# Shared-expert rows as stored high and low parts, a reordered opening and a split last product, in an adaLN block with a top-2 mixture of experts

## The chip, the cores and the metric

The kernel runs on one core of one Trainium2 chip. The metric is the device time of one execution in microseconds (us). A core has five engines that run their own instruction streams and wait for each other by semaphores: TensorE (PE, matrix products; its weight loads are shown as PEld), VectorE (DVE), ScalarE (ACT), GpSimd (POOL), and SyncE (SP), which here only issues DMA transfers. PE's results land in eight PSUM banks of 128 x 512 fp32; everything else that an engine reads is in SBUF.

## The reference, cut to what matters

Everything is fp32 and is computed with nearly fp32 accuracy.

```
x: 2048 x 512;  mod = silu(c) @ wmod -> sa, ca, ga, sb, cb, gb (512 each)
h  = layernorm(x) * (1 + ca) + sa
x  = x + ga * (tanh(h @ B.T) @ C.T + D * h)                 # 256 states
h  = layernorm(x) * (1 + cb) + sb
scores = sigmoid(h @ gate_w.T); pick 2 of 8 experts by scores + bias
w      = the two scores, normalised to sum 1
routed = sum of w_k * W2_k(silu(h @ W1_k) * (h @ W3_k))      # hidden width 352
shared = sw2(silu(h @ sw1.T) * (h @ sw3.T))                  # hidden width 704
out = x + gb * (routed + shared)
```

The shared expert of width 704 is computed as two experts of width 352, A and B, so that A, B and the eight routed experts all have the same shapes.

## The kernel before, in words

A tile is 128 rows (tokens); there are NT = 16 tiles, in NP = 8 pairs. Each fp32 product is made of three products of rounded operands: with a = ah + al and b = bh + bl (`high` is a Copy that rounds to fp32r, `low` is the subtraction of what is left), it is ah*bh + ah*bl + al*bh. So whatever goes into a product needs its high and its low part in SBUF.

The work has three stages.

*Stage A* (function `body`, iterations `it` = 0 to 10). A software pipeline over the pairs: in iteration `it`, pair `it` is normalised, pair `it-1` is transposed (`turn_t`) and its states are computed (`states`), pair `it-2` gets the output of the attention-like part (`attention`), is normalised again and its rows are written to DRAM (`hs`), pair `it-3` is transposed (L1037), split into high and low parts (`xah`, `xal`; `high_a` on ACT, `lows_a` on DVE) and goes through expert A, and pair `it-4` is routed: its rows are fetched back from `hs` and scattered to the DRAM tensor `xs`, where each expert has its own region (`scatter`, four indirect DMAs of POOL). Iteration 3 is the first with an expert in it; what comes before it (L1088 to L1111) is called the opening here.

*Steps* (function `step`, section letters B, S, C). Every step takes one tile through one expert of width 352: `up`, 24 products of 352 columns into banks 2 and 3; `down` of the step before, 9 products of 512 columns; and `turn_g`, three transposes of the hidden values. ACT computes the silu (L873) and the high part of the turned hidden values (L881), DVE their product with the other half (`gbuf`, L1653) and the low part (L1668). In the order of PE the `down` of a step is thus one step late, which gives ACT and DVE the time of an `up`.
- B: four steps, tiles 0 to 3 through shared expert B, while the routing table is finished (`table_rows`, `table_rest` on DVE, semaphores `s_row` and `s_tab`) and the first routed expert's weights come in.
- S: 36 steps (for these inputs) over the routed rows in `xs`; the results are written to the DRAM tensor `ys`.
- C: twelve steps, tiles 4 to 15 through shared expert B. Each one ends with the output: POOL gathers the tile's two rows per token from `ys` (`gather`), DVE combines them with the shared result and x (`finish`, four operations), SP stores. Tiles 0 to 3 are combined beside them in `rowb` (`gather_first`, `finish_first`). I number the C steps k = 0 to 11.

In all 52 steps the tile's rows come by a DMA from DRAM (`hs` in B and C, `xs` in S) into `xin`; PE transposes them (`turn`, four transposes, L929), ACT takes the high part (L722), DVE the low part (L1387).

The weights: POOL fetches each expert's 4.3 MB twice (once to be kept as `raw`, once rounded, `whi`) and computes the low part (L536), into one of two slots.

SP's queue is one list in program order: a DMA that waits holds up all behind it. At the end of stage A this list is: tiles 0 and 1 for B, the rows of pairs 6 and 7 for the scatter (`rows_of_pair`), tiles 2 and 3 for B, and then the rows of the first routed tiles, which wait for all scatters (L450 to L457).

## Time and profile before

| | us |
|---|---|
| median of three runs | 567.3 (567.28 to 568.34) |
| the profiled execution, its own time | 568.31 |
| its span, first to last instruction | 566.6 |
| PE busy in the span | 545.8 |
| DVE, POOL, ACT busy | 301.5, 263.2, 181.1 |

The granted clock of PE was 0.994 of full speed over the span. Stage A ends and B begins at about 205 us of the span, S begins at about 233, C at about 477, and the last store is issued at 564.2. A busy time is the sum of the instructions' own times with overlaps taken once; PE works on several instructions at a time, so what one costs is read from the distance between starts, and not from its length.

### The profile page before, as it was taken

To read this page: it belongs to the slowest core of one execution; us is meant where nothing else is said; L and a number is where in the kernel's file an instruction comes from. 1 tells how busy PE (TensorE), PEld (TensorE's weight loads), DVE (VectorE), ACT (ScalarE), POOL (GpSimd) and SP (SyncE) were. 2 spreads that over 40 slices of the span, in tenths; PEclk is the share of its full clock that TensorE was granted. 3 is DMA by queue.
4 is the path that set the end of the run, shared out by engine and by line. 5 is a ranking of instruction groups with operands and counts; after the bars stand their busy time and mean duration, and the time that the engine had idled before them with its cause. 6 is when DMAs were issued, how large, how long until landed. Compare 5 with 4: busy or idle time off the path is not lost.

```text
span 566.6 us, 11166 instructions
## 1 busy us (share of the span) xinstructions
PE 545.8 (96%) x3184; PEld 490.3 (87%) x3185; DVE 301.5 (53%) x631; ACT 181.1 (32%) x347; POOL 263.2 (46%) x221
## 2 busy tenths in 40 slices
PE   8997799999999999999999999999999999999995
PEld 3666688988999999899999999999999999889994
DVE  3788776696677667632222222222222222479886
ACT  1444346345443442133222322232222322222210
POOL 2599886677667456443053430053535100245531
PEclk9998999999999999999999999999999999999998
DMA  8999245331332597566255754267676222367744
GB/s 306 395 330 333 75 153 219 131 111 74 111 122 103 175 331 292 185 225 223 95 185 203 278 183 178 90 215 267 214 259 206 91 74 74 112 208 221 225 157 137
DMA packets 41113, 107.19 MB, mean 189 GB/s; under 512 B 4224, under 2 KB 4224, under 8 KB 41088
## 3 DMA queue, kind: packets, MB, share of 16 engines
q1 hardware_dynamic: 28288, 54.44, 27.3%
q0 software_dynamic: 12800, 52.43, 26.8%
q8 instruction: 14, 0.23, 0.2%
q14 instruction: 11, 0.09, 0.1%
HBM read 76.19 MB, written 30.67 MB: 189 GB/s over the span
## 4 chain that ended last, share of the span: by engine, by line
PE 82%; POOL 6%; DVE 5%; issue 3%; DMA 2%; ACT 1%; SPq 0%; DVEq 0%; POOLq 0%
PE bank L946 15%; PE bank L947 14%; PE bank L948 14%; PE bank L962 8%; PE bank L960 8%; PE bank L961 8%; PE bank L929 5%; PE bank L967 4%; PE bank L898 2%; PE bank L900 2%; PE bank L899 2%; DMA x_all<-wmod 2%; POOL x_all L552 1%; POOL tmpa L544 1%; POOL tmpa L549 1%
## 5 line engine op out<-in xcount | busy, mean ns | idle before, releaser
L946 PE MATMUL bank<-whi,thi 128*128 (+1 forms) x416 | 139.0, 334 | 0.0
L947 PE MATMUL bank<-wlo,thi 128*128 (+1 forms) x416 | 134.6, 324 | 0.0
L948 PE MATMUL bank<-whi,tlo 128*128 (+1 forms) x416 | 134.3, 323 | 0.0
L536 POOL TENSOR_TENSOR wlo<-raw,whi 128x1408 f32 (+3 forms) x24 | 79.7, 3334 | 87.2 <-DMA whi<-w_all 75.0
L960 PE MATMUL bank<-whi,gth 128*128 (+1 forms) x204 | 80.9, 396 | 2.4 <-DVE gtl L1668 1.3
L962 PE MATMUL bank<-whi,gtl 128*128 (+1 forms) x204 | 80.6, 395 | 0.0
L961 PE MATMUL bank<-wlo,gth 128*128 (+1 forms) x204 | 79.9, 391 | 0.0
L1653 DVE TENSOR_TENSOR gbuf<-s,bank 128x352 f32<-128x352 f32 x52 | 27.1, 521 | 98.5 <-ACT s L873 97.6
L947 PEld LDWEIGHTS bank<-wlo,thi 128*128 128x128 f32 x416 | 78.5, 189 | 0.0
L946 PEld LDWEIGHTS bank<-whi,thi 128*128 128x128 f32 x416 | 78.5, 189 | 0.0
L948 PEld LDWEIGHTS bank<-whi,tlo 128*128 128x128 f32 x416 | 78.3, 188 | 0.0
L1668 DVE TENSOR_TENSOR gtl<-bank,gth 128x384 fp32r<-128x384 f32 x52 | 29.0, 557 | 82.4 <-ACT gth L881 82.4
L873 ACT ACTIVATE s<-bank 128x352 f32<-128x352 f32 x52 | 24.2, 465 | 152.1 <-PE bank L948 152.1
L881 ACT ACTIVATE gth<-bank 128x384 fp32r<-128x384 f32 x52 | 25.5, 490 | 104.1 <-PE bank L967 104.1
L696 POOL DMA_INDIRECT tbuf<-ys_rows,idx x12 | 11.4, 954 | 77.9 <-issue 45.5
L962 PEld LDWEIGHTS bank<-whi,gtl 128*128 128x128 f32 x204 | 38.4, 188 | 8.8
L960 PEld LDWEIGHTS bank<-whi,gth 128*128 128x128 f32 x204 | 38.4, 188 | 8.6 <-issue 2.9
L1387 DVE TENSOR_TENSOR tlo<-bank,thi 128x512 fp32r<-128x512 f32 x52 | 35.8, 689 | 15.6 <-ACT thi L722 15.3
L961 PEld LDWEIGHTS bank<-wlo,gth 128*128 128x128 f32 x204 | 38.5, 188 | 6.0
L946 PE MATMUL bank<-whi,xah 128*128 128x360 f32 (+1 forms) x128 | 42.4, 331 | 0.1
L929 PE MATMUL bank<-cst,h 128*128 128x128 f32 x272 | 40.6, 278 | 1.4 <-DVE gtl L1226 1.4
L947 PE MATMUL bank<-wlo,xah 128*128 128x360 f32 (+1 forms) x128 | 41.6, 325 | 0.0
(201 smaller groups left out, 970.3 us busy)
## 6 DMA issues: line engine op xcount, KB each, us to landing
raw<-w_all POOLq DMA_DIRECT2D x8, 2176.0 KB, 10.4
whi<-w_all POOLq DMA_DIRECT2D x16, 704.0 KB, 11.5
h<-xs_rows SPq DMA_DIRECT2D x36, 256.0 KB, 2.7
ys_rows<-tmpa SPq DMA_DIRECT2D x36, 256.0 KB, 2.0
x_all<-wmod SPq DMA_DIRECT2D x6, 1024.0 KB, 9.9
whi<-w_all POOLq DMA_DIRECT2D x8, 768.0 KB, 4.6
hs_rows<-h SPq DMA_DIRECT2D x8, 512.0 KB, 2.9
h<-hs_rows SPq DMA_DIRECT2D x16, 256.0 KB, 2.7
```

Of the source, the lines that this page charges most:

```text
L536: pool.tensor_tensor(wlo[:, bass.ds(off + (SH + a), b - a)], raw[:, a:b], whi[:, bass.ds(off + (SH + a), b - a)].bitcast(F32), ALU.subtrac ...
L881: act.activation(gth[:, :], bank[4][:, 0:FP], ACT.Copy).then_inc(q["S", "ghi"], 1)
L929: mm = pe.transpose(dst[:, k * P:(k + 1) * P], src[:, k * P:(k + 1) * P], ident)
L946: pe.matmul(dst, xh[:, j, a], wh, start=(m == 0), stop=False)
L947: pe.matmul(dst, xh[:, j, a], wl, start=False, stop=False)
L948: mm = pe.matmul(dst, xl[:, j, a], wh, start=False, stop=(m == KD - 1))
L960: pe.matmul(dst, gth[:, a], wh, start=(m == 0), stop=False)
L961: pe.matmul(dst, gth[:, a], wl, start=False, stop=False)
L962: mm = pe.matmul(dst, gtl[:, a], wh, start=False, stop=(m == KF - 1))
L1387: dve.tensor_tensor(xbl[:, j, :], src[:, :], xbh[:, j, :].bitcast(F32), ALU.subtract).then_inc(q["S", "xlo"], 1)
L1653: dve.tensor_tensor(gbuf[:, 0:F], s1[:, :], bank[3][:, 0:F], ALU.mult).then_inc(q["S", "g"], 1)
L1668: dve.tensor_tensor(gtl[:, :], bank[4][:, 0:FP], gth[:, :].bitcast(F32), ALU.subtract).then_inc(q["S", "glo"], 1)
```

## The change

Seven things change; the names are those of the diff.

1. `store_x`: the high and low parts that expert A uses (`xah`, `xal`) are also written to two DRAM tensors `xth` and `xtl`, pair by pair, two DMAs of 512 KB in each of eight iterations of SP's list. `high_a` waits until the pair before is stored.
2. `load_x`: in B and C a tile's two parts (256 KB each) are loaded straight into `xbh` and `xbl` when the `up` two steps before is done. `turn`, `high` and `lows` are left for the 36 routed tiles only (`routed_next`). The loads from `hs` for B and C go.
3. Iteration 3 (`lo == 3`): PE transposes pair 2 after `attention` instead of ahead of the h2 transposes, into banks 6 and 7; ACT and DVE take xah/xal ahead of thi/tlo. The gate weights' high and low parts are taken earlier, in the opening.
4. `routed` (weights of the two experts and positions in `ys`) moves one step forward, from the first S step to the last B step, in two halves.
5. The last two tiles (14, 15) are combined like tiles 0 to 3: their `ys` rows are gathered early into free buffers (`gather_first`, now six tiles in steps k = 2 to 7), weighted by ACT (`weigh`) and combined with x by DVE (`combine`, three operations, two of them in each of the steps k = 3 to 11). What is left behind their `down` is one multiplication and one addition (`finish_last`).
6. The last `up` does its first half's products first (`apart`), so that the silu can start after 12 of 24; the transposes of the last hidden values stand inside the `down` before; the last `down` is computed in two halves of 256 columns in two banks (`down_last`), each finished and stored on its own.
7. The first C tile's last two DVE operations (`finish_out`) come one step later, behind the `gbuf` of step 2.

```diff
@@ SP
+            def load_x(t, j):
+                for dst, src in ((xbh, xth), (xbl, xtl)):
+                    sp.dma_start(dst[:, j, :].bitcast(F32), src[t * P:(t + 1) * P, :]).then_inc(q["C", "xin"][j], 16)
+
+            def store_x(p):
+                sp.wait_ge(q["A", "xlo"], p * 2 + 2)
+                for dst, src in ((xth, xah), (xtl, xal)):
+                    sp.dma_start(dst[bass.ds(p * 2 * P, 2 * P), :].rearrange("(b p) d -> p b d", p=P),
+                                 src[:, :, :].bitcast(F32)).then_inc(s_xts, 16)
...
                 if lo == NP + 2:
+                    sp.wait_ge(s_stp, NP)
+                    sp.wait_ge(s_xts, 32 * (NP - 1))
+                    for t in range(2):
+                        load_x(t, t)
                     sp.wait_ge(s_nat, NP * 16)
-                    sp.wait_ge(s_h2T, NP)
-                    for t in range(2):
-                        load(hs, t, t * P)
...
                     rows_of_pair(p, 0)
+                if live(3, lo, hi):
+                    store_x(it - 3)
...
-            def next_c(s, j, tile):
-                sp.wait_ge(q["S", "xt"], s * 2 + (j + 2 + NB))
-                load(hs, 1 - j, tile * P)
+            def next_c(k):
+                if k < NT - NB:
+                    sp.wait_ge(q["S", "up"], iters * 2 + (NB + k - 1))
+                    load_x(NB + k, k % 2)
...
             for t in range(2, NB):
-                sp.wait_ge(q["S", "xt"], t - 1)
-                load(hs, t % 2, t * P)
+                sp.wait_ge(q["S", "up"], t - 1)
+                load_x(t, t % 2)
+            sp.wait_ge(s_xts, 32 * NP)
+            sp.wait_ge(s_h2T, NP)
             sp.wait_ge(s_pad, 48)
             sp.wait_ge(s_scat, 64 * (NP - 1))
@@ ACT
                 if lo > 3:
                     act.wait_ge(q["A", "up"], p * 2)
+                    act.wait_ge(s_xts, p * 32)
...
+            def weigh(t):
+                act.wait_ge(s_brow[t], 32)
...
+                act.activation(rowb[t][:, 0, :], rowb[t][:, 0, :], ACT.Identity, bias=zrow[:, 0:1],
+                               scale=wts[:, at_:at_ + 1, 0]).then_inc(s_b0, 1)
@@ TensorE
+            def down_last(i, off):
+                pe.wait_ge(q["S", "glo"], i * 2 + 2)
+                for h in range(2):
+                    dst = bank[6 + h][:, h * (D // 2):(h + 1) * (D // 2)]
+                    for m in range(KF):
...
+                        mm = pe.matmul(dst, gtl_b[:, a], wh, start=False, stop=(m == KF - 1))
+                    mm.then_inc(s_ldn, 1)
@@ TensorE, step
-                if not last and not early:
-                    next_turn()
+                if routed_next(i, j, c, sec):
...
+                    turn(i + j, 1 - j, bank[j])
...
-                up("S", i, j, off, [NW + 1, NW + 2] if sec == "B" else need_up)
+                up("S", i, j, off, [NW + 1, NW + 2] if sec == "B" else need_up,
+                   i + 1 if sec == "B" else c + 1 if sec == "C" else None, last)
@@ VectorE
-            def finish_first(t, half):
...
+            def combine(t, part):
+                y0, y1, at_ = rowb[t][:, 0, :], rowb[t][:, 1, :], FIRST_LAST[t]
+                if part == 0:
+                    dve.wait_ge(s_b0, t + 1)
+                    dve.scalar_tensor_tensor(y1, y1, wts[:, at_:at_ + 1, 1], y0, ALU.mult, ALU.add).then_inc(s_b2, 1)
+                elif part == 1:
...
+            def finish_last(t, h, cuts):
+                w = slice(h * (D // cuts), (h + 1) * (D // cuts))
+                y, r, n = bank[5 + t + h][:, w], rowb[NB + t][:, 1, w], t + h + 1
+                dve.tensor_tensor(y, y, mods[:, 5, w], ALU.mult).then_inc(s_lx, 1)
+                dve.wait_ge(s_lx, n)
+                dve.wait_ge(s_b4, NB + t + 1)
+                dve.tensor_tensor(r, y, r, ALU.add).then_inc(s_ly[t], 1)
```

The next two pieces are SP's list from the end of stage A to the first rows of the routed tiles (L392 is `rows_of_pair`; TENSOR_LOAD reads a row number from the routing table), before and then after:

```order
DMA h<-hs_rows 128x512 [waits s_h2T,s_nat]
DMA h<-hs_rows 128x512
DMA tmpa<-hs_rows 128x2x512 [waits s_xd]
DMA mods<-hs_rows 128x2x512 [waits s_scat]
DMA h<-hs_rows 128x512 [waits xt_S] x2
TENSOR_LOAD ti [waits s_scat2,s_row,s_scat,s_pad]
```

```order
DMA thi<-xt_high 128x512 [waits s_xts,s_stp]
DMA tlo<-xt_low 128x512
DMA thi<-xt_high 128x512
DMA tlo<-xt_low 128x512
DMA tmpa<-hs_rows 128x2x512 [waits s_xd,s_nat]
DMA mods<-hs_rows 128x2x512 [waits s_scat]
DMA xt_high<-xah 128x2x512 [waits xlo_A]
DMA xt_low<-xal 128x2x512
DMA thi<-xt_high 128x512 [waits up_S]
DMA tlo<-xt_low 128x512
DMA thi<-xt_high 128x512 [waits up_S]
DMA tlo<-xt_low 128x512
```

Between the rows of pair 7 (`mods<-hs_rows`) and the table read there were two transfers of 256 KB; now there are two stores of 512 KB and four loads of 256 KB, and the table read waits for the stores too.

The second place is PE's list between the last `down` but one and the end, before and then after (`L962`/`L1040` is the third product of a piece; rows that only repeat are left out):

```order
L962 MATMUL bank<-whi,gtl 128x512
L967 MATMUL bank<-cst,gbuf 128x128 [waits g_S]
L967 MATMUL bank<-cst,gbuf 128x128 x2
L960 ISA [waits y_C,glo_S]
L960 MATMUL bank<-whi,gth 128x512
```

```order
L1038 MATMUL bank<-whi,gth 128x512
L1039 REGISTER_ALU
L1039 MATMUL bank<-wlo,gth 128x512
L1040 MATMUL bank<-whi,gtl 128x512
L1208 REGISTER_ALU
L1045 MATMUL bank<-cst,gbuf 128x128 [waits g_S]
L1045 MATMUL bank<-cst,gbuf 128x128 x2
L1038 ISA
L1038 MATMUL bank<-whi,gth 128x512
```

The transposes stood behind all nine products of that `down`; now they stand behind the first three, and six products follow them.

## Rows read from the trace of the kernel before

**Rows 1.** The page, part 1: busy us, share of the span, instructions.
```profile
PE 545.8 (96%) x3184; PEld 490.3 (87%) x3185; DVE 301.5 (53%) x631; ACT 181.1 (32%) x347; POOL 263.2 (46%) x221
```
**Rows 2.** Timeline of PE, last C steps: start us, us, engine, line, operation.
```profile
543.78 0.49 PE L967 MATMUL bank<-cst,gbuf 128*128 128x128 f32 x3
...
550.48 0.49 PE L967 MATMUL bank<-cst,gbuf 128*128 128x128 f32 x3
...
556.78 0.49 PE L967 MATMUL bank<-cst,gbuf 128*128 128x128 f32 x3
```
**Rows 3.** Timeline of iterations 3 and 4, several engines.
```profile
47.37 1.06 PE L929 MATMUL bank<-cst,tbuf 128*128 128x128 f32 x8 [4.21 <-issue]
...
59.65 3.80 POOL L552 TENSOR_TENSOR x_all<-x_all,tmpa 128x1024 f32<-128x1024 f32 x1
...
65.25 1.41 DVE L1484 SCALAR_TENSOR_TENSOR h<-h,rs,mods 128x512 f32<-128x512 f32 x2 [0.59 <-POOL rs L579]
...
67.28 0.47 PE L960 MATMUL bank<-whi,gth 128*128 128x512 f32 x1 [1.13 <-DVE gtl L1226]
```
**Rows 4.** Timeline of PE, B steps and the first S step.
```profile
225.94 0.63 PE L929 MATMUL bank<-cst,h 128*128 128x128 f32 x4
...
232.39 0.49 PE L967 MATMUL bank<-cst,gbuf 128*128 128x128 f32 x3
...
240.21 0.55 PE L967 MATMUL bank<-cst,gbuf 128*128 128x128 f32 x3 [0.96 <-DVE gbuf L1653]
```
**Rows 5.** Timeline of SP from 200 us: the rows of pair 7, the first routed rows.
```profile
201.85 0.38 SPq L392 DMA_DIRECT2D mods<-hs_rows  x1
...
223.22 0.35 SPq L389 DMA_DIRECT2D h<-xs_rows  x1
```
**Rows 6.** Stretches: us, busy (x) of PE, PEld, DVE, ACT, POOL, PEclk, DMA share, GB/s.
```profile
40.00:60.00 20.00, 14.59 (x70) 11.58 (x69) 17.19 (x25) 8.03 (x15) 19.44 (x16) 0.91 0.78 287
...
204.00:210.00 6.00, 6.00 (x42) 5.55 (x41) 4.55 (x15) 3.57 (x5) 3.07 (x4) 1.00 1.04 400
...
216.00:220.00 4.00, 4.00 (x27) 3.54 (x26) 3.86 (x17) 1.66 (x4) 1.60 (x2) 1.00 1.03 410
220.00:224.00 4.00, 4.00 (x26) 3.91 (x25) 3.56 (x14) 0.76 (x2) 2.60 (x1) 1.00 0.50 183
```
**Rows 7.** DMA queues, 203 to 205, then 207 to 209 us: packets, MB, share.
```profile
q0 software_dynamic: 180, 0.78, 97.6%
...
q0 software_dynamic: 125, 0.53, 68.6%
q1 hardware_dynamic: 124, 0.25, 35.1%
```
**Rows 8.** Timeline around the first C tiles, several engines.
```profile
492.26 0.75 DVE L1617 SCALAR_TENSOR_TENSOR tmpa<-tbuf,wts,bank 128x512 f32<-128x512 f32 x1 [2.74 <-DMA xtf<-ys_rows,idx]
...
496.45 0.55 PE L967 MATMUL bank<-cst,gbuf 128*128 128x128 f32 x3 [1.69 <-DVE gbuf L1653]
...
499.88 1.22 POOL L702 DMA_INDIRECT raw<-ys_rows,idxb  x1 [0.30 <-DVE tmpa L1620]
...
504.36 0.49 DVE L1598 TENSOR_SCALAR raw<-raw,wts 128x512 f32<-128x512 f32 x1 [1.97 <-DMA raw<-ys_rows,idxb]
```
**Rows 9.** Timeline of the tail.
```profile
558.53 0.49 PE L960 MATMUL bank<-whi,gth 128*128 x1 [1.26 <-DVE gtl L1668]
...
561.20 0.74 DVE L1617 SCALAR_TENSOR_TENSOR tmpa<-tbuf,wts,bank 128x512 f32<-128x512 f32 x1
...
563.49 0.69 DVE L1624 TENSOR_TENSOR tmpa<-tmpa,x_all 128x512 f32<-128x512 f32 x1
```
**Rows 10.** Stage A: SP's rows of a pair, ACT's next high parts.
```profile
104.20 0.40 SPq L392 DMA_DIRECT2D mods<-hs_rows  x1
...
115.53 1.09 ACT L729 ACTIVATE xah<-bank 128x512 fp32r<-128x512 f32 x2
```
**Rows 11.** The page, part 6: DMA issues, KB each, us to landing.
```profile
hs_rows<-h SPq DMA_DIRECT2D x8, 512.0 KB, 2.9
```

More of the change, by code:

```diff
@@ L60 @@
           ("par", E + 4)]
+NL = 2
+FIRST_LAST = [*range(NB), *range(NT - NL, NT)]
+WEIGH_AT = [3, 4, 6, 7, 9, 10]
 COL, _at = {}, 0
@@ L311, in routes, with routed_next @@
             return lo - 4 >= 0 and hi - 4 < NP
+        def routed_next(i, j, c, sec):
+            if sec == "B":
+                return i * 2 + j == NB - 1
+            return sec == "S" and not (c == -1 and j == 1)
         def steps(eng, step, known, unrolled=False):
@@ L322, in steps @@
                     step(i, j, None, "S")
-            with eng.Fori(CB + 2, iters + CB) as i:
+            with eng.Fori(CB + 2, iters + (CB - 1)) as i:
                 for j in range(2):
                     step(i, j, None, "S")
+            for j in range(2):
+                step(iters + (CB - 1), j, -1, "S")
             first = NP - 1 if unrolled else CB + 2
@@ L707, in _ @@
                 gather(CB, j)
-            for c in range(CB + 1, NP):
+            for c in range(CB + 1, NP - 1):
                 for j in range(2):
@@ L887, in known @@
                 return pairs_of_b(act)
-            steps(act, step, known)
+            steps(act, step, known, True)
         @block.tensor
@@ L955, in down @@
                 for m in range(KF):
+                    if between and m == 1:
+                        between()
                     a = slice(m * P, (m + 1) * P)
@@ L1132, in step @@
                         before = pe.snap(off_b[1 - j], min_val=0, max_val=WSZ)
-                def next_turn():
-                    if first:
-                        pe.wait_ge(q["A", "y"], NT - 1)
-                    else:
-                        pe.wait_ge(q["A", "y"], NT)
-                        pe.wait_ge(q["S", "xlo"], i * 2 + j)
+                if routed_next(i, j, c, sec):
+                    pe.wait_ge(q["A", "y"], NT)
+                    if sec == "S" and not (isinstance(i, int) and i + j == CB):
+                        pe.wait_ge(q["S", "xlo"], (i - CB) * 2 + j)
                     turn(i + j, 1 - j, bank[j])
-                if not last and not early:
-                    next_turn()
                 if first:
@@ L1165, in step @@
                         pe.wait_ge(q["C", "y"], c * 2 + (j - 2 - NB))
-                    down("S", i - 1 + j, 1 - j, before, 5, 2 * NW if before is WSZ else need_dn[1 - j])
+                    down("S", i - 1 + j, 1 - j, before, 5, 2 * NW if before is WSZ else need_dn[1 - j],
+                         (lambda: hidden_turned(i, j)) if last else None)
                 if sec == "B" and i + j == CB:
@@ L1556, in _, with routed @@
                 body(it, it, it)
-            def routed():
+            def routed(half):
                 n = NT * 2
@@ L1629, in step @@
                 first, last = sec == "B" and i + j == 0, sec == "C" and c * 2 + j == NT - 1
-                early = sec == "B" and i == 0
-                def next_lows():
-                    if not first:
-                        dve.wait_ge(q["S", "up"], i * 2 + j)
+                if routed_next(i, j, c, sec):
+                    dve.wait_ge(q["S", "up"], i * 2 + j)
                     lows(i + j, 1 - j, bank[j])
-                if not last and not early:
-                    next_lows()
                 if sec == "B" and i * 2 + j == 1:
@@ L1653, in step @@
                 dve.tensor_tensor(gbuf[:, 0:F], s1[:, :], bank[3][:, 0:F], ALU.mult).then_inc(q["S", "g"], 1)
-                m = (c - CB) * 2 + j - 3 if sec == "C" else -1
-                if 0 <= m < 2 * NB:
-                    finish_first(m // 2, m % 2)
-                if early:
-                    next_lows()
+                if b3:
+                    routed(1)
+                m = (c - CB) * 2 + j - 3 if sec == "C" else -2
+                if m == -1:
+                    finish_out(CB, 0)
+                if m >= 0:
+                    for n in range(2 * m, 2 * m + 2):
+                        combine(n // 3, n % 3)
                 if sec == "B" and i * 2 + j == 1:
@@ L1673, in step @@
                     offsets(CB, j)
-                if sec == "C" and c + j > CB:
+                if last:
+                    dve.wait_ge(q["S", "dn"], i * 2 + j)
+                    finish_last(0, 0, 1)
+                elif sec == "C" and c + j > CB:
                     finish(i - 1 + j, c - 1 + j, 1 - j, held[0])
-                    if not last:
+                    if c + j < NP - 1:
                         offsets(c + j, 1 - j)
@@ L1684, in _ @@
             iters = steps(dve, step, known, True)
-            finish(iters + (NP - 1), NP - 1, 1, iters)
+            for h in range(2):
+                dve.wait_ge(s_ldn, h + 1)
+                finish_last(1, h, 2)
 def kernel(L0_attn_x, L0_attn_B, L0_attn_C, L0_attn_D, L0_ffn_gate_w, L0_ffn_router_bias, L0_ffn_W1,
```

220 lines of the change are left out of this document (131 added, 89 removed).

## The prediction

> **What bounds the kernel.** I read page part 1 first: PE is busy 545.8 of 566.6 us [rows 1], so at most 20.8 us can come from waiting and the rest only from work that PE no longer does. The timeline of PE in the C steps then prices that work. From the transposes of the hidden values of one step to those of the next it is 6.70 us with the tile's own transposes in between (543.78 to 550.48) and 6.30 without (550.48 to 556.78, the last step, whose rows were turned before) [rows 2]. So a `turn` costs 0.40 us of PE's time, though its four transposes are recorded as 0.6 long. The rest of the reading was for places where PE does not set its own pace, because there removed PE work gives nothing: the opening, B, the first C steps and the tail.
>
> **The opening (part 3 of the change).** PE stands 4.2 us until the transposes at 47.37 [rows 3]. In the new order the h2 transposes and `attention` go ahead, about 3.5 us of work put into that hole, and the first `up` can start some 3 us earlier. But PE is not the last link here. POOL works through its list without a break (it is busy 19.4 of the 20 us from 40 to 60 [rows 6], then 3.8 us on x_all at 59.65), DVE's second normalisation waits for POOL at 65.25, and PE's first `down` waits for the DVE operation behind it at 67.28 [rows 3]. Nothing on POOL's list moves. What PE gains before 60 us it waits at 67. I take 0; the bounds are -2 (POOL is disturbed less) and +1 us. For the former speaks that 128x1024 takes POOL 3.8 us here. The Trainium skill ("SBUF — State Buffer", Who interferes with whom) says that a DVE instruction with two SBUF inputs contends with a GpSimd instruction that reads SBUF; the moved DVE subtractions of weights are of that kind. They then meet the POOL instruction before instead of this one, so by that rule too the sum stays, at 0.
>
> **Stores in stage A (part 1).** Per iteration two DMAs of 512 KB more. SP's list lets them go behind the rows of a pair, at 104.2 in one iteration; the next high part, which now waits for them, is due at 115.53 [rows 10]. A 512 KB store lands in 2.9 us [rows 11], so two are there by about 109.5. Cost 0, hidden by 6 us of slack; without that cover it would be paid in each of five iterations (a rival below).
>
> **B (parts 1 and 2).** Four turns go, 1.6 us, and PE would come to the first turn of a routed tile at 224.3 instead of 225.94 [rows 4]. But its rows are loaded at 223.22 [rows 5], once all scatters have landed, and are there 2.7 us later: PE already comes just in time. So the 1.6 us are lost at once, and the question is when the scatters land now. From 204 to 220 us the DMA engines are full, at 400 and 410 GB/s, and only after that does it fall to 183 [rows 6]: expert 0's weights, the last two pairs' scatters and SP's small loads all run there. SP's list now puts two stores (1.05 MB) right behind the rows of pair 7 of 201.85 [rows 5], and doubles the loads of tiles 2 and 3 (0.52 MB more). 1.57 MB at 0.40 MB per us are 3.9 us if everything waits for everything. The scatters are not last in that crowd (the third piece of the weights is issued after them), so I take half, 2.0 us: row load at 225.2, there at 227.9, that is 1.9 us later than 225.94. Tile 2's parts are behind the stores too; I estimate them at 220, 2 us later than PE wants them, which is inside the same 1.9 since PE would have to wait at 224 anyway. B costs +1.9. Bounds: -1.6 (no wait at all) and +5.3 (below).
>
> The Trainium skill ("DMA: Bandwidth & Descriptors", Queues, rings and completion order) says that each DMA engine takes turns between the queues it has work for. The packet counts of 207 to 209 us are like that, 125 to 124, those of 203 to 205 are not: SP's rows were issued at 201.85 and its queue moved nothing [rows 7]. By equal turns the stores are through at about 218 and the sum is the one above; if POOL's queue goes ahead as in the second row, tile 2's parts come at 223 and B costs 3.6 before any effect on the clock.
>
> **First S step (part 4).** 232.39 to 240.21 is 7.8 us, 1.1 above a step, since DVE computes `routed` before PE's transposes can go [rows 4]. Moved into B's last step, where DVE has 1.9 us free before `gtl` and where `lows` are gone, it is hidden. Gain 1.1; bounds 0 and 1.4.
>
> **C steps (parts 2, 5, 7).** Twelve turns go. Two lie ahead of the first C tile's shared result: 0.8. From there the ends are fixed by the gathers. DVE begins the first `finish` at 492.26, when they have landed, and PE's transposes of k = 2 come at 496.45 after 1.69 of waiting [rows 8]. Now two operations of 0.78 instead of four, no `lows` (0.68), casts 0.2 and `gbuf` 0.5 stand between: 494.65 on the old clock, 1.8 earlier (0.8 of it turns). Then `weigh(0)` has to wait for its gathers. They are issued 2 us earlier than now, the last at 497.95, and take 4.5 us (499.88 to 504.36 [rows 8]): 502.4. Behind it on ACT waits the high part of k = 3, on DVE `combine`, `gtl` and the whole `finish` of tile 2: 0.6 + 1.5 + 0.6 + 3.0 + 0.2 + 0.5 puts `gbuf` of k = 4 at 508.7, 1.5 us late (now this wait is 0.9). From 508.75 seven steps of 6.30 make 552.85 against 556.78 [rows 2], a gain of 3.9. DVE then has per step 0.5 + 1.5 + 0.6 + 3.0 + 0.2 = 5.8 of work in 6.3 us, and the DMAs of k = 2 to 7 move 1.84 MB per step, 290 GB/s; both fit, barely. Gain 0.8 + 3.9 = 4.7; bounds 1.5 and 5.7.
>
> **The tail (parts 5 and 6).** The last `down` starts at 558.53 after 1.26 of waiting, DVE starts the last `finish` at 561.20 and ends it at 564.18 [rows 9]: 5.65 us. The silu now runs inside the `up`, and the transposes come 0.75 us after its end instead of 2.1; `gtl` then waits for the two `combine` operations (1.5 us), so the `down` starts 0.85 earlier. I take its 18 products of 256 columns to last as long as nine of 512; if each cost a fixed part on top, say a tenth of the 2.1 us in all, the gain would shrink by 0.2. DVE behind it has 2 x 0.42 instead of 2.98 us: 2.15 less. Gain 3.0; bounds 1.5 and 3.8.
>
> **Sum.** 0 + 1.9 - 1.1 - 4.7 - 3.0 = -6.9 us against the profiled execution's 568.3, so 561.4. That execution is 1.0 above the median of the three runs, so against the median 560.4.
>
> **Rivals.**
> - *B is crowded worse.* Tile 2's parts come only when POOL's transfers are through, 223.2; turn of the routed tile at 229.5, +3.6. PE then stands 5 us, as long as in the opening, and there 20 us had a granted clock of 0.91 [rows 6], that is 3.6 us at 1.2 instead of 2.4 GHz: 1.8 us more. Total +5.3: 563.8. For it: the 97.6% of POOL's queue [rows 7]; against: SP's queue had its share from 205 on.
> - *B is free.* If scatters and parts come early enough, B gives 1.6: 556.9; if only the parts do, B is 0: 558.5. Against: the stretch is full to the last GB/s.
> - *C bound by DVE or gathers.* Steps k = 4 to 10 stay at 6.7: +2.8, 563.2. For it: DVE's 5.8 of 6.3, and gathers of four tiles' halves per step.
> - *The opening's gain survives*: 558.5. Against: POOL's unbroken list.
> - *Slower.* Stores in stage A hold `high_a`. Both must land within 11 us of 104.6; the price is each us beyond, five times. If they took 13.5 us the loss would be 2.5 x 5 = 12.5, against the gains 573. For it: in a full stretch SP's queue can stand still, as from 203 to 205 [rows 7]. Against: in stage A the engines are used by a third.
>
> **Chances.** Forecast 0.46, B worse 0.16, B free or even 0.16, C bound 0.10, opening 0.05, slower 0.07. The forecast's own range is 558.5 to 562.5; with the neighbours 556.3 to 564.8. A change under 0.2% (1.1 us) can't be told from none: faster 0.90, same 0.03, slower 0.07.
>
> **What would show it.** In the new profile: PE steps of 6.3 us in C; a PE wait of 1 to 3 us in B, ended by tile 2's parts or by the transposes' rows; no wait of PE in the first S step; PE's first `down` still near 67 us behind POOL; the last store issued about 3 us sooner after the last `up`. The prediction is wrong if the clock falls in B, if PE waits in every C step, or if ACT waits for the stores in stage A.

## The result, and the profile after

The changed kernel takes 569.8 us in the median of 20 runs, the kernel before 568.3 in 20: a ratio of 1.0032, 95% interval 1.002 to 1.0043. So it is 0.3% slower, where 7 us faster was forecast. The profiled execution of the changed kernel has 571.33 us of its own against 568.31 (spans 569.7 and 566.6); it is 1.5 us above the median of its kernel, so the account below, which is of that execution, has 3.1 us to explain and not 1.5. The runs of the changed kernel also lie further apart, 568.0 to 572.4 us against 567.3 to 569.5.

The transposes of the hidden values (`turn_g`, L967 before, L1045 now) come once a step, and the two traces can be laid side by side by them. Between the same two of them TensorE does the same work but for the turns. That gives this account (us, after less before, profiled executions):

| stretch | forecast | measured | from |
|---|---|---|---|
| opening and stage A up to the step at 191 | 0 | -0.7 | 191.81, now 191.08 |
| last step of stage A | 0 | +1.4 | 198.31, now 198.99 |
| B | +1.9 | +7.5 | 232.39, now 240.56 |
| first S step | -1.1 | -1.1 | 240.21, now 247.30 |
| routed steps | 0 | +1.5 | 467.83, now 476.46 |
| C up to the last tile but one | -4.7 | -1.9 | 550.48, now 557.18 |
| tail (with the last step) | -3.0 | -3.6 | 566.6, now 569.7 |
| sum | -6.9 | +3.1 | |

The three rows of the kernel before that are not shown yet, timeline of PE (start us, us, engine, line, operation):

```profile
191.81 0.49 PE L967 MATMUL bank<-cst,gbuf 128*128 128x128 f32 x3
198.31 0.49 PE L967 MATMUL bank<-cst,gbuf 128*128 128x128 f32 x3
...
467.83 0.49 PE L967 MATMUL bank<-cst,gbuf 128*128 128x128 f32 x3
```

The same of the changed kernel, with the first `down` and every wait of PE that the account rests on:

```profile
66.45 0.47 PE L1038 MATMUL bank<-whi,gth 128*128 128x512 f32 x1 [1.33 <-DVE gtl L1305]
...
191.08 0.49 PE L1045 MATMUL bank<-cst,gbuf 128*128 128x128 f32 x3
192.93 0.40 PE L1007 MATMUL bank<-whi,xah 128*128 128x360 f32 x1 [1.28 <-DVE xal L1472]
198.99 0.49 PE L1045 MATMUL bank<-cst,gbuf 128*128 128x128 f32 x3
...
225.60 0.63 PE L1007 MATMUL bank<-whi,thi 128*128 128x352 f32 x1 [6.45 <-issue]
...
233.86 0.49 PE L1045 MATMUL bank<-cst,gbuf 128*128 128x128 f32 x3
234.19 0.60 PE L984 MATMUL bank<-cst,h 128*128 128x128 f32 x4
240.56 0.49 PE L1045 MATMUL bank<-cst,gbuf 128*128 128x128 f32 x3
247.30 0.49 PE L1045 MATMUL bank<-cst,gbuf 128*128 128x128 f32 x3
...
476.46 0.49 PE L1045 MATMUL bank<-cst,gbuf 128*128 128x128 f32 x3
...
510.06 0.42 PE L1007 MATMUL bank<-whi,thi 128*128 x1 [1.71 <-issue]
515.17 0.49 PE L1038 MATMUL bank<-whi,gth 128*128 x1 [1.00 <-DVE gtl L1760]
518.53 0.55 PE L1045 MATMUL bank<-cst,gbuf 128*128 128x128 f32 x3 [1.02 <-DVE gbuf L1742]
...
550.88 0.49 PE L1045 MATMUL bank<-cst,gbuf 128*128 128x128 f32 x3
557.18 0.49 PE L1045 MATMUL bank<-cst,gbuf 128*128 128x128 f32 x3
```

The 6.45 us at 225.60 are put down to "issue", that is to nothing that PE's rows name: it is the wait for tile 2's parts. SP's rows there, and the stretches of the changed kernel (us, busy of PE, PEld, DVE, ACT, POOL, PEclk, DMA share, GB/s), answer to [rows 5, 6]. SP first:

```profile
203.49 0.81 SPq L425 DMA_DIRECT2D xt_high<-xah  x1
204.34 1.08 SPq L425 DMA_DIRECT2D xt_low<-xal  x1
209.92 0.35 SPq L420 DMA_DIRECT2D thi<-xt_high  x1
210.69 0.35 SPq L420 DMA_DIRECT2D tlo<-xt_low  x1
...
227.99 1.48 SPq L412 DMA_DIRECT2D h<-xs_rows  x2
```

Then the stretches:

```profile
216.00:220.00 4.00, 3.08 (x15) 2.11 (x13) 3.83 (x20) 0.95 (x2) 3.01 (x4) 1.00 1.04 413
220.00:224.00 4.00, 0.00 (x0) 0.00 (x0) 2.42 (x8) 0.00 (x0) 3.19 (x2) 0.97 1.04 413
224.00:226.00 2.00, 0.40 (x1) 0.43 (x2) 0.00 (x0) 0.00 (x0) 2.00 (x1) 0.50 1.09 420
226.00:230.00 4.00, 4.00 (x15) 4.00 (x15) 0.00 (x0) 0.00 (x0) 1.60 (x2) 0.50 0.39 138
```

The parts were issued at 209.92 and 210.69 and used at 225.60. Where the kernel before had 183 GB/s from 220 on, the engines are now full until 226. And PE came back at a granted clock of 0.50, that is 1.2 GHz: from 225.60 to 233.86 are 8.3 us for an `up` and a `down` that take 6.0 elsewhere (3.9 and 2.1), 2.3 us for the clock. The wait and the clock are 8.8 us; the turns that are gone give 1.3 of them back, and 7.5 are left. The end of stage A is a wait for a store: ScalarE stood for the store of pair 6's low parts, DVE and PE behind it (timeline of ACT, changed kernel).

```profile
191.47 1.09 ACT L777 ACTIVATE xah<-bank 128x512 fp32r<-128x512 f32 x2 [2.64 <-DMA xt_low<-xal]
```

In the tail the last `down` starts without the wait of 1.26 us that stood there [rows 9]. PE of the changed kernel:

```profile
564.08 0.38 PE L1022 MATMUL bank<-whi,xah 128*128 x1
```

and DVE's last two operations, short ones now:

```profile
566.50 0.43 DVE L1692 TENSOR_TENSOR bank<-bank,mods 128x256 f32<-128x256 f32 x1
566.97 0.42 DVE L1695 TENSOR_TENSOR mods<-bank,mods 128x256 f32<-128x256 f32 x1
```

From the start of the last `down` to the end of the span are 5.6 us, before 8.1.

### The profile page after: what moved, and what is told of

The parts are those of the page before. It is cut to its first block, busy times and chain, and to the rows that moved or that the text cites. A ratio compares the mean times of both kernels' runs of the same rounds, so it can differ in the third digit from the quotient of the medians.

```text
span 569.7 us, 11068 instructions
## 1 busy us (share of the span) xinstructions
PE 543.4 (95%) x3129; PEld 487.3 (86%) x3130; DVE 286.6 (50%) x612; ACT 176.3 (31%) x337; POOL 263.5 (46%) x221
## 4 chain that ended last, share of the span: by engine, by line
PE 79%; POOL 7%; issue 5%; DMA 4%; DVE 3%; ACT 1%; SPq 0%; POOLq 0%; DVEq 0%; ACTq 0%
PE bank L1007 14%; PE bank L1009 14%; PE bank L1008 14%; PE bank L1038 8%; PE bank L1040 7%; PE bank L1039 7%; PE bank L984 4%; PE bank L1045 4%; PE bank L955 2%; PE bank L953 2%; PE bank L954 2%; DMA x_all<-wmod 2%; POOL tmpa L595 1%; DMA xt_low<-xal 1%; POOL x_all L598 1%
## 5 line engine op out<-in xcount | busy, mean ns | idle before, releaser
L1040 PE MATMUL bank<-whi,gtl 128*128 (+1 forms) x201 | 79.0, 393 | 0.0
L1040 PEld LDWEIGHTS bank<-whi,gtl 128*128 128x128 f32 x201 | 37.8, 188 | 8.9
L1039 PEld LDWEIGHTS bank<-wlo,gth 128*128 128x128 f32 x201 | 37.8, 188 | 5.8
L553 POOL DMA_DIRECT2D whi<-w_all x21 | 11.4, 552 | 66.5 <-PE bank L1009 66.3
L1009 PE MATMUL bank<-whi,xal 128*128 128x360 f32 (+1 forms) x128 | 41.6, 325 | 0.0
L1045 PEld LDWEIGHTS bank<-cst,gbuf 128*128 128x128 f32 x204 | 25.9, 140 | 16.1 <-issue 4.3
```

What stands on the lines that cost most here:

```text
L1009: mm = pe.matmul(dst, xl[:, j, a], wh, start=False, stop=(m == KD - 1))
L1039: pe.matmul(dst, gth[:, a], wl, start=False, stop=False)
L1040: mm = pe.matmul(dst, gtl[:, a], wh, start=False, stop=(m == KF - 1))
L1045: mm = pe.transpose(dst[:, m * P:(m + 1) * P], gbuf[:, m * P:(m + 1) * P], ident)
```

## The experiments

Sixteen kernels in four groups (e; f; g with t; h); the runs of a group share a chip and the runs of the kernel before. They build on each other: f1 is made from e4, f2 from f1, f3 and f4 from f2, g1, t1 and t2 from f3, h3 and h4 from g1; e1 to e3 and h1 are made from the changed kernel, t3 and h2 from the kernel before. Ratios are to the kernel before, with their 95% interval. The profile of each is one execution.

| run | ratio | interval | median us | runs from, to |
|---|---|---|---|---|
| changed kernel | 1.0032 | 1.002 to 1.0043 | 569.8 | 568.0, 572.4 |
| e1_store7_late | 0.9948 | 0.9934 to 0.9962 | 566.6 | 566.0, 567.9 |
| e2_tiles23_early | 0.9993 | 0.9973 to 1.0013 | 569.4 | 564.8, 571.8 |
| e3_c_order | 1.0023 | 1.0012 to 1.0034 | 571.1 | 569.7, 572.9 |
| e4_all_three | 0.9926 | 0.9909 to 0.9944 | 564.9 | 562.7, 567.4 |
| f1_c_gathers_as_changed | 0.9931 | 0.9913 to 0.995 | 565.7 | 563.9, 567.5 |
| f2_c_paced | 0.9929 | 0.9908 to 0.995 | 564.7 | 560.7, 567.6 |
| f3_counts_folded | 0.9901 | 0.988 to 0.9921 | 563.4 | 559.8, 566.3 |
| f4_last_undivided | 0.9923 | 0.9902 to 0.9943 | 565.7 | 563.7, 567.0 |
| g1_old_addresses | 0.983 | 0.9814 to 0.9846 | 558.1 | 556.3, 558.6 |
| t1_first_rows_by_sp | 0.9893 | 0.9861 to 0.9926 | 561.3 | 559.4, 563.3 |
| t2_small_x_loads | 0.9846 | 0.9827 to 0.9866 | 558.8 | 557.6, 559.8 |
| t3_before_more_loads | 1.0011 | 0.9995 to 1.0026 | 568.6 | 566.2, 570.2 |
| h1_changed_old_addresses | 1.001 | 0.9994 to 1.0027 | 570.0 | 567.9, 573.7 |
| h2_before_shifted | 1.003 | 1.0016 to 1.0044 | 571.4 | 570.2, 572.5 |
| h3_late_group_shifted | 0.9881 | 0.9853 to 0.991 | 563.8 | 561.0, 565.3 |
| h4_tables_shifted | 0.9886 | 0.9851 to 0.9922 | 564.0 | 560.0, 565.8 |

### B: what crowds it

**e1_store7_late.** The last pair's stores go behind the first routed rows, and the wait for them ahead of these rows goes too:

```
 if live(3, lo, hi) and lo < NP + 2:      # was: if live(3, lo, hi)
     store_x(it - 3)
...
 for n in range(3): ... load(xs, n % 2, row)
 store_x(NP - 1)
```

> The last pair's two stores (1.05 MB) go out behind the first routed rows' loads instead of at 203.5 us. In the trace of the changed kernel the parts of B's tile 2, issued at 209.9 and 210.7, were waited for until 225.6 (6.45 us of idle TensorE), and both DMA queues carried packets without a gap from 203 to 226. Theory (queue turns): the two queues carry about equal shares, so taking 1.05 MB from SyncE's queue ahead of the parts brings them 5 us earlier (1.05 MB at about 200 GB/s): the wait falls from 6.45 to about 1.5 us, with part of the slow clock behind it gone: 569.8 - 5 to - 7 = 563 to 565. Rival (all 16 engines are simply full, order does not matter): 1.05 MB at 400 GB/s, 2.6 us: 567.2. Rival (the parts wait for something else than bytes, such as the issue behind the expert's weights on GpSimd's queue): no change, 569.8.

Timeline of PE in e1:

```profile
218.28 0.55 PE L1047 MATMUL bank<-cst,gbuf 128*128 128x128 f32 x3 [0.28 <-issue]
224.65 0.49 PE L1047 MATMUL bank<-cst,gbuf 128*128 128x128 f32 x3
226.94 0.63 PE L986 MATMUL bank<-cst,h 128*128 128x128 f32 x4 [1.81 <-DMA h<-xs_rows]
```

The third tile's `up` runs without a wait, so its parts, issued at 209.4 and 209.8, were there some 6.8 us or more sooner than 225.6. What is left is 1.81 us for the first routed rows, loaded at 224.17 (before: 223.22 [rows 5]). At the first S step e1 is 7.2 us ahead of the changed kernel (240.13 against 247.30), but only 4.5 of them are left at the last tile but one (552.71 against 557.18): C lost the rest, with waits of 1.99, 0.97, 1.02, 0.98 and 0.47 us. The ratio falls by 0.84%, 4.8 us, just under the 5 to 7 expected. The theory that the order in the queue decides holds; 2.6 us, which the bytes alone would give, is too little. Its "equal shares" were not equal in bytes. From 209 to 219 us of the changed kernel the packets of SP's queue and of POOL's are served one to one, and SP's are the smaller ones. From 211 to 213 us there (queue, packets, MB, share):

```profile
q0 software_dynamic: 113, 0.55, 78.6%
q1 hardware_dynamic: 112, 0.20, 31.2%
```

SP's packets are of 1.8 KB, POOL's of 4.9 KB, and SP's queue moves 0.10 MB per us where all together move 0.38. The Trainium skill ("DMA: Bandwidth & Descriptors", Queues, rings and completion order) says that each DMA engine takes turns between its queues by the packet. These counts agree with that; those of 221 to 223 us, 131 against 207, are not one to one. What stands ahead in SP's own queue therefore costs more than its bytes over the full rate.

**e2_tiles23_early.** Tiles 2 and 3 into `bhi` and `blo`, which nobody reads any more:

```
+for t in range(2, NB):
+    for dst, src in ((b23h, xth), (b23l, xtl)):
+        sp.dma_start(dst[:, t - 2, :].bitcast(F32), src[t * P:(t + 1) * P, :]).then_inc(s_x23[t - 2], 16)
```

> The parts of B's tiles 2 and 3 are loaded right behind those of tiles 0 and 1 (at about 192 us) into the buffers of the state weights, which are free by then; nothing else is changed, the last pair's stores stay at 203.5. Theory: TensorE no longer waits at B's third step: 6.45 us of idle time and some 2.3 us of slow clock behind it go. What is late next is the first routed rows' load, behind the last scatter (landed about 227 in the changed kernel, 1 MB less traffic ahead of it now): a wait of 1 to 3 us at the turn of the first routed tile. 569.8 - 8.7 + 1 to 3 = 562 to 564. Rival (the expert's weights by GpSimd's queue, not the parts, set the end of B: TensorE would wait for them at about 226 to 230 anyway): about 567.

Timeline of PE in e2:

```profile
224.66 0.49 PE L1051 MATMUL bank<-cst,gbuf 128*128 128x128 f32 x3
228.14 1.09 PE L987 MATMUL bank<-cst,h 128*128 128x128 f32 x4 [2.98 <-DMA h<-xs_rows]
```

The wait at the third step goes and 2.98 us come back at the first routed tile, with the clock gone down again (its turn is 1.09 us long, not 0.6). In the trace the first S step is at 242.56, 4.7 us before the changed kernel's and still 2.35 behind the kernel before; over the runs the gain is only 0.4%, 2.2 us, and they lie 7 us apart. In the trace, too, C took back 2.5 of the 4.7 us (555.03 against 557.18 at the last tile but one). With tile 2 out of the way B ends on the first routed rows, loaded at 225.34 once the last scatter has landed. The expectation named that link with 1 to 3 us and left out the clock behind it: from 224.66 to 235.86 are 11.2 us, 4.5 more than a step, of which 1.5 are the clock.

### C: order, bursts, and releases that come late

**e3_c_order** and **e4_all_three.**

```
+for k in range(2): gather_first(0, k)             # right behind gather(CB, 0), gather(CB, 1)
...
+if k == 1: next_c(4)                              # ahead of store_out of the first tile
...
+own = p == NP - 1                                 # e4 alone, with e1 and e2: pair 7 in chi, clo
```

> Stage C alone: the first early tile's two gathers are issued right behind the first two C gathers, where GpSimd idled from 498.6 to 501.6, the others are spread out; SyncE issues the loads for C's fifth tile ahead of the first store of an output tile, behind which they waited from 499.7 to 503.1. Theory: the three waits of TensorE at 510.06 (1.71), 515.17 (1.00) and 518.53 (1.02 us) go: 569.8 - 3.7 = 566.1. Rival (the queues are full there whatever the order, 323 to 378 GB/s from 504 to 512): the waits only move to the next steps, under 1 us of gain: 569.

> All of it together, and the last pair of stage A in buffers of its own (those of the output weights), so that ScalarE no longer waits for the store of the pair before (2.64 us of idle ScalarE, 1.28 us of idle TensorE at 192.93). Theory: the gains add up: 8.7 less 0 to 2 for the first routed rows, 3.7 in C and 1.3 at the end of A: 569.8 - 13 = 557 (555.5 to 558.5), 11 us under the kernel before. Rival (weights and scatters of the first expert bound B's end): 560 to 562.

Both miss. By the ratios e3 gains 0.5 us on the changed kernel, which is inside the noise, and e4 6.0, where 3.7 and 13 were expected. The three waits are gone, and one of 3.15 us stands in their place. Timeline of e4, several engines ("remote": the release came from nothing that the rows show at that time):

```profile
490.30 0.32 PE L1027 MATMUL bank<-whi,tlo 128*128 x1
...
494.78 0.46 ACT L940 ACTIVATE s<-bank 128x352 f32<-128x352 f32 x1 [7.52 <-remote]
...
494.78 0.33 SPq L423 DMA_DIRECT2D thi<-xt_high  x1
...
495.86 0.90 PE L1063 MATMUL bank<-cst,gbuf 128*128 128x128 f32 x3 [3.15 <-issue]
```

The last matmul of the `up` starts at 490.30, and the Silu and SP's load both need nothing but this `up`. In every C step of the kernel before the Silu starts 0.36 us after that row; here both start at 494.78. I call this a late release: of the result, not of the matmuls, for PE's `down` went on at 490.46. The wait that follows also brings the clock down: in e3 PE ran at 0.50 from 503 to 509 us, and the step behind the wait took 9.0 us instead of 6.3; in e4 it took 7.9. So the stall cost 5.9 us in e3 and 4.8 in e4, more than the three waits that it replaced. The wait of 1.28 us at the end of A is gone in e4 and in the kernels made from it.

**f1_c_gathers_as_changed** and **f2_c_paced.** f1 takes e4's gathers back to the changed kernel's order; the cut is f2 against f1:

```
-WEIGH_AT = [3, 4, 6, 7, 9, 10]
+WEIGH_AT = [4, 5, 6, 7, 9, 10]
...
-if n < NB + NL: gather_first(n, 0), gather_first(n, 1)
+t = {0: 0, 1: 1, 2: 2, 3: 3, 5: 4, 6: 5}.get(n)   # f2: three combine parts in C steps 4 and 5
```

> e4_all_three with C's gathers in the order of the changed kernel again; only SyncE's load for C's fifth tile stays ahead of the first output store. e4 and e3 both showed one wait of 3.15 to 3.18 us of TensorE ahead of the third C step's turn of the gated rows, with ScalarE and SyncE released together some 4 us after the product that they waited for; both had eight gathers issued back to back there. Theory (the early first gathers made a burst of eight, which holds everything up): that wait is gone, and what is left are the two waits on the combination of the first early tile (1.0 and 1.0 us, ScalarE held behind its gather): C costs 1.5 us less than in e4, 563.5. Rival (the third C step would stall whatever the order): 565.

> f1 with the combination of the first two early tiles one C step later each (ScalarE's part at C steps 4 and 5 instead of 3 and 4, three VectorE parts in these two steps), the gathers of the fifth and sixth a step later. Theory: ScalarE no longer stands before a gather that is under way; no C step waits, each takes 6.28 us: 2 us less than f1, 561.5. Rival (VectorE, 5.6 us a step and 6.3 in the two with three parts, or full queues set C's pace): no gain over f1.

f1's third C step no longer stalls (6.30), and the combination of the first early tile costs 2.17 and 1.02 us there; but its runs are no faster than e4's. f2 has no wait over 0.8 us in C in its profile, which is 560.74 us, the fastest of its six runs; the others go to 567.6. So in the median the pacing is not shown to gain anything over f1, and something that varies from run to run by up to 7 us was left. Both profiles have several late releases in C.

**f3_counts_folded.** `(i - CB) * 2 + (j + 1)` written as `i * 2 + (j + 1 - 2 * CB)`.

> f2 with the semaphore counts of the routed steps written as i*2 plus a constant, as the kernel before has them, instead of (i - 2)*2 plus a constant. In every kernel with this change the routed step takes 6.74 us, with its 24 first-product matmuls 162.3 ns apart; in the kernel before 6.69 and 160.0 to 160.5. Over 34 steps that is 1.6 us. Theory (one more register operation ahead of the step shifts the phase in which its matmuls fall in): back to 6.69, 1.6 us less than f2. Rival (the spacing comes from somewhere else, as the time at which the loop is entered): 6.74 stays, no difference.

The routed step stays at 6.74 us (299.79, 306.53, 313.27): the theory falls. The lower median is within f2's scatter.

**f4_last_undivided.** `down_last` in one piece of 512 columns, `finish_last` and its store in one.

> f2 with the last product in one piece of 512 columns and its output finished and stored in one piece: the part of the tail that the halves alone are worth. From the rows of the changed kernel: with one piece VectorE's two operations of 0.69 start at about the product's end and the store of 256 KB follows; with halves the last two are 0.42 and 0.42 and the store has half the bytes. Theory: 0.5 us later end than f2, plus 0.2 to 0.5 for the larger last store: 0.5 to 1.0. Rival (the halves cost TensorE what they save VectorE, 18 matmuls of 120 ns against 9 of 230): no difference.

From the last `turn_g` to the end of the span: 8.3 us (557.12 to 565.4), in f2 7.5 (551.62 to 559.1). In these two profiles the halves are worth 0.8 us, as the theory had it; the runs of f4 and f2 can't be told apart.

### Addresses

**g1_old_addresses.** The allocator rounds to 32 bytes. `idxb` has grown from 32 to 48 bytes a partition, so all that is allocated behind it lies 32 bytes higher.

```
-idxb = sb("idxb", [P, 2 * (NB + NL)], U32)
+hole = sb("hole", [P, 2 * NB], U32)
...
+idxb = sb("idxb", [P, 2 * (NB + NL)], U32)        # behind big3, the last tensor
```

> f3 with the longer index tensor (48 instead of 32 bytes a partition) allocated last, so that every other tensor lies at the SBUF address that it has in the kernel before. Theory (the 16 bytes by which later tensors were shifted cost the first product 2 ns a matmul): the routed step falls from 6.74 to 6.69 us and the kernel gains 1.6 us over f3. Rival (the spacing of 162.3 ns against 160.0 to 160.5 comes from how the step's instructions fall in, not from addresses): 6.74 stays.

Timeline of PE, a routed step of the changed kernel:

```profile
301.22 0.49 PE L1045 MATMUL bank<-cst,gbuf 128*128 128x128 f32 x3
307.96 0.49 PE L1045 MATMUL bank<-cst,gbuf 128*128 128x128 f32 x3
```

and one of g1:

```profile
298.32 0.49 PE L1062 MATMUL bank<-cst,gbuf 128*128 128x128 f32 x3
305.02 0.49 PE L1062 MATMUL bank<-cst,gbuf 128*128 128x128 f32 x3
```

6.74 and 6.70 (6.69 in the mean of 34). The ratio falls from 0.9901 to 0.983, 4 us, more than the 1.6 expected, and the runs lie within 2.3 us instead of 6.5. g1 has no late release, where f3's profile has five in C. Nothing is left in C of g1 but one wait of PE:

```profile
523.34 0.42 PE L1024 MATMUL bank<-whi,thi 128*128 x1 [0.47 <-DMA tlo<-xt_low]
```

g1 beats both kernels, by 1.7% the one before.

**t1_first_rows_by_sp, t2_small_x_loads, t3_before_more_loads.** t1: `gather_first` replaced by `sp.dma_start(rowb[tt][:, kk, :], ys[...])`; t2: `n = 64 if t >= NB else D` in `load_x`; t3, on the kernel before:

```
+sp.dma_start(xah[:, :, :].bitcast(F32), hs[0:2 * P, :]...).then_inc(s_more, 16)   # at each next_c
```

> f3 with the early tiles' rows loaded by twelve plain loads of 256 KB on SyncE's queue in place of twelve gathers on GpSimd's (the rows are those of fixed places, so these six output tiles are not the reference's); the bytes are the same. In C of every kernel with the change, and not in the kernel before, ScalarE and SyncE were let go 0.4 to 4.3 us after the product that they wait for had ended in the rows. Theory A (back-to-back gathers on GpSimd do it): the late releases go and C's steps are all 6.28. Theory B (the bytes do it, 285 GB/s over the step): they stay, and C takes as long as in f3.

> f3 with the loads of C's x parts cut to 64 of 512 columns (what is computed from the rest is the tile before's), so that SyncE moves 64 KB instead of 512 KB a step; the gathers stay. Theory B (bytes): C's steps at 6.28 and no late release; the executions scatter as little as those of the kernel before (under 2 us), about 1 to 3 us faster than f3 in the median. Theory A (gathers on GpSimd): the late releases stay.

> The kernel before with one more load of 512 KB (into a buffer that is free there, nobody reads it) at each of C's steps. It has no late release in C now, at 189 GB/s. Theory B (bytes): at about 270 GB/s late releases of 0.4 to 4 us appear between the end of a product on TensorE and ScalarE's Silu or SyncE's load, and C becomes 2 to 6 us longer. Theory A (dense gathers): C gets longer by under 1.5 us, through later loads of x, and no product's release is late.

t1 has no late release; its only C wait is 1.57 us for a load of x, at 238 GB/s over C, as much as in f3. Bytes alone don't do it: Theory B falls. t2 has none either and no wait at all in C, at 176 GB/s, and its gain over f3 is clear of the noise (t1's is not): Theory A in its plain form falls as well, the gathers were all there. t3 moves 244 GB/s in C instead of the 189 of before (287 from 495 to 545 us), no release is late, and the ratio is 1.0011 with 1 inside. Against f3, then, the late releases are absent when either of the two is taken out. That the two together are what they need is not shown: g1 has both and none is late, and h2, below, has neither.

**h1 to h4.** h1: g1's edit alone on the changed kernel. h2: the kernel before with `pad = sb("pad", [P, 8], U32)` behind `idxb`. h3: g1 with that pad ahead of `xah`; h4: g1 with one ahead of `sw` and one ahead of `xah`.

 Theory: the routed step is 6.69 instead of 6.74 us (1.5 us over the span), and in C no release is late, while the wait for B's third tile (some 8 us with the slow clock) and the SyncE order in C stay: 2 to 5 us faster than the changed kernel, 0.994 to 1.000 of the kernel before. Rival (g1's gain came from the order of its run alone): 1.003 as it was.

> The kernel before with 32 unused bytes a partition behind the index words, so that the tensors from there on are shifted as in the changed kernel; not one instruction differs but in addresses. Theory: the routed step goes from 6.69 to 6.74 us (1.5 us), and C with its gathers gets late releases: 1.003 to 1.008 of the kernel before, with a wider scatter. Rival (the shift matters only together with the change's denser traffic): 1.000.

> g1 with 32 unused bytes ahead of xah, so that xah, xal, s1, sign5, gbuf, gth, gtl and big3 alone are shifted, the small tables and index words not. Theory (it is TensorE's and ScalarE's big operands): 6.74 us a routed step, late releases in C, 4 us slower than g1. Rival (it is the small tables): as g1, 558.

> g1 with 32 unused bytes ahead of the small tables and another 32 ahead of xah: the tables and index words (wts, pos, idx, ti and so on) change places modulo 64 bytes, the big operands from xah on do not (64 bytes of shift). Theory (big operands): as g1, 6.69 us and no late release. Rival (small tables, of which TensorE's and SyncE's registers are loaded): 6.74 us.

Timeline of PE in h2:

```profile
300.82 0.49 PE L968 MATMUL bank<-cst,gbuf 128*128 128x128 f32 x3
307.56 0.49 PE L968 MATMUL bank<-cst,gbuf 128*128 128x128 f32 x3
```

The kernel before, instruction for instruction, goes to 6.74 us a routed step and to 1.003: 32 bytes cost it as much as the whole change did. The profile of h2 also has late releases, four of them in its B and C steps, where the kernel before has none in any step. The longest is in B, before any gather; PE and ACT there:

```profile
215.52 0.32 PE L949 MATMUL bank<-whi,tlo 128*128 128x352 f32 x1
...
217.63 0.46 ACT L874 ACTIVATE s<-bank 128x352 f32<-128x352 f32 x1 [4.74 <-remote]
```

2.11 us instead of 0.36. Two more are in C, at 505.38 and 508.33. So neither the change's x loads nor its gathers are needed. h1 is at 6.69 us a routed step again. Its interval has 1 in it and overlaps the changed kernel's; it is about 0.2% under it, the size of the 1.5 us of the routed steps. In C it waits like the changed kernel and has late releases. PE of h1:

```profile
506.01 0.42 PE L1008 MATMUL bank<-whi,thi 128*128 x1 [2.06 <-DMA tlo<-xt_low]
...
526.09 0.49 PE L1039 MATMUL bank<-whi,gth 128*128 x1 [0.93 <-DVE gtl L1761]
529.45 0.55 PE L1046 MATMUL bank<-cst,gbuf 128*128 128x128 f32 x3 [1.01 <-DVE gbuf L1743]
```

and ACT:

```profile
539.99 0.49 ACT L937 ACTIVATE gth<-bank 128x384 fp32r<-128x384 f32 x1 [4.00 <-remote]
```

The gain of h1 is less than expected. So the addresses are the cause of the slow routed step. In the late releases they have a part by the one profile of h2, and by that of h1 they are not the only cause. h3 (6.74) and h4 (6.72, 300.59 to 307.31) are both slow, by 0.5% or 3 us against g1, and both have late releases. Either edit is enough to slow the step, so "big operands" against "small tables" is not the right cut; in h4 the late group is moved too, by 64 bytes, so it does not show the tables by themselves.

## Why the prediction was wrong

**The clause that failed first is B's +1.9**, bounds -1.6 to +5.3; it measured +7.5, which is 5.6 of the 10.0 us by which the sum is off. C has 2.8 of them, the routed steps 1.5. Three steps of B's clause were off. "1.57 MB at 0.40 MB per us are 3.9 us if everything waits for everything. [...] I take half" priced bytes in a common pool, where SP's own list decides: the stores of 203.49 and 204.34 were directly ahead of tile 2's parts. "I estimate them at 220": they were used at 225.60, and e1, without the stores ahead, has no wait for them. And the third, the rival "B is crowded worse", had the right mechanism, the parts behind a full stretch and the clock behind the wait, but at 223.2 and 1.8 us; it was 225.6 and 2.3. I had read 183 GB/s of 220 to 224 [rows 6] as room; the added 1.57 MB filled it and two us more. The rival got 0.16 and should have had the forecast's place.

**Stage A, 0.** Right for the iterations with 6 us of slack, five of them. Wrong for the last pair: its high parts come early in the same iteration in which pair 6 is stored, and there is no slack: 2.64 us of ACT, 1.28 of PE, +1.4 in all. I priced the wait where it repeats and did not look for the one place where the program's order is another. e4 with buffers of their own removes it (197.46 against 198.31 before and 198.99).

**Opening, 0.** PE's first `down` is at 66.45 against 67.28 [rows 3]: 0.8 us of it survived, 0.7 of them at 191. The moved subtraction of weights (58.61 on DVE before, 56.07 now) meets the POOL operation that I had put it on: x_all takes 2.73 instead of 3.80 us and the operation before it 4.45 instead of 2.50, and x_all ends at 63.45 in both traces. The 0.8 us come from the two small POOL operations behind it (0.20 and 0.70 us instead of 0.64 and 1.09), inside my bounds of -2 and +1.

**First S step, -1.1.** Right: 7.82 became 6.74.

**Routed steps, no term.** Not forecast: 34 steps of 0.045 us. Cause shown by h2 and h1: addresses, not instructions.

**C, -4.7.** The sum itself has a slip: the 494.65 for k = 2 already holds the 0.8 us of the first turns, and 552.85 is worked out from it, so the working gives 3.9; the 0.8 was added twice. The step is right: 6.3 us (550.88 to 557.18). The first tiles were even better, since `gbuf` of k = 2 had no wait any more (501.60, 3.5 us gained since the last routed step where 1.8 was forecast). Two things then went the other way. First, from there to `gbuf` of k = 4 the forecast has two steps and 1.5 us of waiting for `weigh(0)`; it took two steps and 4.3. The load of x for k = 4 went out at 503.06, behind the first output's store, and came at 510.06, a wait of 1.71 us that the forecast does not have. The gather of 505.78 let ACT go only at 512.24; behind it are the waits of 1.00 and 1.02. I had priced that gather at 4.5 us from a trace with 189 GB/s in C; here the engines moved 308 to 402 GB/s from 506 to 514 us. Second, the last six steps took 38.65 us instead of 37.8, with five late releases among them (the Silu of 530.51 comes 1.58 us after its product's last row). The rival "C bound by DVE" did not happen: g1's DVE has three parts in two steps and stays at 6.30.

**Tail, -3.0.** Right, 0.6 too little: -3.6, of it 0.8 for the halves (f4).

**Slower, 0.07**, was given to one mechanism, stores holding `high_a` five times. That did not happen; B, the routed steps, the end of A and C together made it slower, none alone. g1, which has the change without most of these costs, is 9.7 us under the kernel before, where 6.9 were forecast: the gains are there.

**Open.** Why 32 bytes of address cost TensorE 2 ns a matmul (160.0 to 160.5 against 162.3), and which tensor it is. And what holds a release back: it went with dense gathers and x loads together and not with one of them (t1, t2), but it is absent in g1, present in h1 at the old addresses, and present in h2, which is the kernel before with nothing but moved addresses. These are single profiles of kernels whose runs vary; the scatter of the runs does not go with it throughout (e1 had several such rows in its profile, and its runs lie within 2 us). What pacing is worth at the old addresses was not tried.

## What to carry to other kernels

Price an added DMA by what stands behind it on the queue of the engine that issues it, not by its bytes over a shared rate, and look at the stretch that seems to have room: the added bytes end there. Look for the one iteration in which the order is another before calling a repeated wait hidden. When a change resizes a small tensor, keep the addresses of all others, or measure the shift by itself: 32 bytes were as large as the whole verdict here.

## What the runs showed of the hardware that I had not expected

- SBUF addresses: the same instructions take 6.69 or 6.74 us a step, 1.003 in the whole (h2), with all tensors behind `idxb` moved by 32 bytes.
- After 6.45 us without matmuls PE came back at 225.60 at a granted clock of 0.50, until 230: 2.3 us on top of the wait. In e2 2.98 us of waiting already had it (a turn of 1.09 instead of 0.6 us), in h2 1.98 (0.50 from 500 to 502 us), while 2.64 us in f4 did not (1.00 from 226 to 230).
- Late releases: a product ended at about 490.6 in the rows, and two engines that waited for it both started at 494.78, while PE went on (e4). The kernel before has none in the B, S and C steps of its profile; moved by 32 bytes it has four (h2).
- Two queues with work in them were served one to one by packets and not by bytes: 113 packets of 4.9 KB against 112 of 1.8 KB in 2 us, 0.55 against 0.20 MB.
